# Attention products on the whole TensorE array, one PSUM bank per half, and the softmax shift cut as columns

## What is computed

```python
q = einsum('rc,bcn->brn', Wq, x) + bq        # 16 rows
k = einsum('rc,bcn->brn', Wk, x) + bk        # 16 rows
v = einsum('oc,bcn->bon', Wv, x) + bv        # 128 rows
attn = softmax(einsum('bri,brj->bij', q, k), axis=2)
x = gamma * einsum('bcj,bij->bci', v, attn) + x
```

## Time and profile before

| What | us |
|---|---|
| median of 3 runs | 207.81 (207.34 to 209.48) |
| the profiled execution, whole | 206.91 |
| its span, first to last instruction | 205.0 |
| PE, ACT, POOL, DVE busy | 192.7, 161.0, 155.9, 144.8 |

### The profile page before, as it was taken

The page is one execution under the profiler, slowest core; times in us unless marked ns, Lnnn a source line. Parts: engine busy times, 40 slices in busy tenths (PEclk is TensorE's granted clock), DMA queues, the critical chain, the costliest instruction groups (busy, mean ns, idle before and its releaser), DMA issues.

```text
span 205.0 us, 3349 instructions
## 1 busy us (share of the span) xinstructions
PE 192.7 (94%) x1217; PEld 124.8 (61%) x1217; DVE 144.8 (71%) x146; ACT 161.0 (79%) x237; POOL 155.9 (76%) x88
## 2 busy tenths in 40 slices
PE   7999999999889998999999999999999899998792
PEld 2433254555578656647875867775676768777570
DVE  0297688996999789689866897879874876532202
ACT  2229659889999989997999979699979997558420
POOL 1330000686499999998978988999999999999990
PEclk9998599999999999999999999999999999999998
DMA  6808000030040004002100004001410101001011
GB/s 184 328 14 205 0 2 3 13 93 0 3 106 0 2 6 102 0 6 51 51 3 3 0 2 107 0 6 51 102 53 5 51 0 51 30 28 51 3 51 51
DMA packets 3746, 9.31 MB, mean 45 GB/s; under 512 B 532, under 2 KB 916, under 8 KB 3732
## 3 DMA queue, kind: packets, MB, share of 16 engines
q1 hardware_dynamic: 3732, 9.12, 15.0%
HBM read 2.69 MB, written 2.10 MB: 23 GB/s over the span
## 4 chain that ended last, share of the span: by engine, by line
PE 51%; ACT 15%; POOL 15%; DVE 9%; issue 6%; DMA 2%; SPq 0%; POOLq 0%; DVEq 0%; ACTq 0%
PE out_psum L570 20%; POOL attn_lo L310 10%; PE ring L535 8%; ACT ring L344 7%; ACT attn L362 6%; PE out_psum L600 5%; POOL attn_hi L305 4%; PE out_psum L571 4%; DVE neg_max L435 4%; PE ring L521 4%; PE ring L511 3%; PE ring L556 3%; DMA qk_swapped<-qk 2%; PE ring L499 2%; DVE x_all L460 1%
## 5 line engine op out<-in xcount | busy, mean ns | idle before, releaser
L310 POOL TENSOR_TENSOR attn_lo<-attn,attn_hi 128x1024 fp32r<-128x1024 f32 x48 | 116.2, 2441 | 8.9 <-ACT attn_hi L369 8.0
L435 DVE TENSOR_REDUCE neg_max<-ring 128x1 f32<-128x1024 f32 x64 | 76.5, 1220 | 14.3 <-PE ring L537 13.5
L344 ACT ACTIVATE ring<-ring,neg_max 128x1024 f32<-128x1024 f32 x64 | 69.7, 1088 | 13.1 <-DVE neg_max L435 12.4
L362 ACT ACTIVATE attn<-ring 128x1024 f32<-128x1024 f32 x64 | 63.5, 1024 | 15.8 <-PE ring L558 15.4
L305 POOL TENSOR_SCALAR attn_hi<-attn 128x1024 fp32r<-128x1024 f32 x32 | 36.2, 1138 | 27.9 <-ACT attn L362 27.4
L556 PE MATMUL ring<-qk,qk_swapped 64*128 64x512 f32 x64 | 30.1, 485 | 2.7 <-ACT attn L362 2.0
L570 PE MATMUL out_psum<-attn_hi,v_hi 64*128 64x512 f32 x96 | 30.7, 399 | 1.5 <-DVE x_all L463 1.2
L571 PE MATMUL out_psum<-attn_hi,v_hi 64*128 64x512 f32 x96 | 30.7, 399 | 0.0
L558 PE MATMUL ring<-qk_swapped,qk 64*128 64x512 f32 x64 | 30.5, 491 | 0.0
L570 PE MATMUL out_psum<-attn,v 64*128 64x512 f32 x64 | 30.0, 588 | 0.0
L571 PE MATMUL out_psum<-attn,v 64*128 64x512 f32 x64 | 30.0, 588 | 0.0
(11 more groups left out here) (48 smaller groups left out, 322.4 us busy)
## 6 DMA issues: line engine op xcount, KB each, us to landing
qk_swapped<-qk SPq DMA_DIRECT2D x16, 256.0 KB, 3.7
out_dram<-x_all SPq DMA_DIRECT2D x8, 256.0 KB, 2.0
x_all<-x_in SPq DMA_DIRECT2D x3, 512.0 KB, 7.1
...
qk<-shift_rows SPq DMA_DIRECT2D x7, 8.0 KB
qk_swapped<-shift_rows SPq DMA_DIRECT2D x7, 8.0 KB
```

What stands on the lines that cost most here:

```text
L310: nc.gpsimd.tensor_tensor(attn_lo[:, k - 1], attn[:, k], attn_hi[:, k - 1].bitcast(fp32), ALU.subtract).then_inc(lo_made, 1)
L344: nc.scalar.activation(e[:], e[:], ACT.Exp, bias=max_column(s, i), accum_out=row_sum[s][:, i:i + 1]).then_inc(sum_made, 1)
L362: nc.scalar.activation(attn[:, k], ring_tile("ET", s, k)[:].rearrange("p (a n) -> p a n", a=2), ACT.Exp).then_inc(attn_made, 1)
L435: nc.vector.tensor_reduce(max_column(s, i), ring_tile("E", s, i)[:], axis=AX.X, op=ALU.max, negate=True).then_inc(max_made, 1)
```

## The change

Counts of entries in the order lists:

| Entry | before | after |
|---|---|---|
| PH, native PV, other PV (PE) | 48, 16, 48 | 46, 18, 46 |
| warm matmuls in the list (PE) | 31 | 23 |
| steps in PE_ORDER from full-array to row-split entries or back | 61 | 124 |
| of these, into a warm entry | 13 | 7 |
| hi, lo on POOL | 32, 48 | 33, 36 |
| hi on ACT; lo on DVE | 16; 0 | 13; 10 |
| v_hi on ACT, on POOL | 8, 0 | 1, 7 |
| v_lo on DVE, on POOL | 8, 0 | 2, 6 |
| mask and stack on DVE, on POOL | 7, 0 | 6, 1 |
| place on SP | 9 | 8 |

- Products (`WHOLE`, all stages): one matmul with 128 contraction rows and 512 columns in place of the pair, into the bank of the half. A half's products wait for the finish of the same half of the stage before. DVE's finish is one instruction.
- Stage 0 has four native k (0, 1, 4, 7).
- Shift: DVE subtracts the logarithm from the negative maximum and cuts the columns in two fp32r parts (`parts`, three small instructions); one fp32r matmul transposes them, and one copy brings the rows out of PSUM. ACT's copy of the maxima is gone.
- In stage 0, first half (`ADDED`), the rows are not placed by DMA: each of the four ETs is followed by eight small matmuls of 128 columns (64 rows each, in pairs) that add them. Their selection matrices and the identity are a new input (`units`), loaded by SP after `late` and rounded on POOL.
- QK.1 leaves PSUM by one ACT instruction (`evac`), and POOL masks and stacks it.
- All five lists are rearranged.

```diff
 PAIRS = [0, 1, 2, 3, 1, 2, 3, 0]
+NATIVES = [(0, 1, 4, 7), (0, 7), (0, 7), (0, 7), (0, 7), (0, 7), (0, 7), (0, 7)]
...
 BY_HALVES = (0,)
+ADDED = (0,)
+WHOLE = (0, 1, 2, 3, 4, 5, 6, 7)
+FROM_SBUF = (1,)
...
 PE_ORDER = """
-raw.0.0.0 raw.0.1.1 QK.1.0.2 E.0.2.0 E.0.1.1 warm.0.8 E.0.0.2 E.0.3.0 warm.0.2 E.0.4.1 warm.0.1 E.0.5.2 E.0.7.0
...
-ET.4.5.0 PH.3.6 PH.3.4 E.5.6.2 ET.4.7.0 PV.3.6 E.6.3.1 PV.3.4 PV.3.5 V.5.0.0 shift.5.1.2 PH.4.1 E.6.0.1 ET.4.0.0
-PH.4.3 PH.4.2 E.6.7.2 ET.4.6.0 PV.4.2 E.6.5.1 PV.4.3 PV.4.1 E.6.1.0 PV.4.0 ET.5.3.2 QK.7.0.1 ET.5.1.2 PH.4.6
...
-PH.7.2 PV.7.3 PV.7.0 PV.7.1 PV.7.2 ET.7.4.0 ET.7.7.2 PH.7.5 PH.7.6 PH.7.4 PV.7.7 PV.7.5 PV.7.6 PV.7.4
+raw.0.0.0 raw.0.1.1 QK.1.0.2 E.0.2.0 E.0.0.1 E.0.3.2 warm.0.4 E.0.1.0 E.0.7.1 E.0.4.2 warm.0.2 E.0.6.0 warm.0.2
+E.0.5.1 warm.0.1 shift.0.0.2 warm.0.4 E.1.0.0 E.1.7.2 warm.0.3 QK.2.0.1 ET.0.2.0 shift.0.1.2 warm.0.3 ET.0.1.2
...
+shift.5.1.2 PV.3.6 ET.4.1.0 E.6.7.2 ET.4.4.1 PV.4.0 V.5.0.0 ET.4.5.1 E.6.4.2 PH.4.6 E.6.1.0 E.6.2.1 PH.4.2 PH.4.1
+QK.7.0.2 ET.5.0.1 ET.5.1.0 PV.4.7 PV.4.1 ET.5.2.1 ET.5.6.2 E.6.3.0 PV.4.2 PH.4.3 PV.4.6 E.6.5.2 E.6.6.1 PH.4.5
...
+PV.7.3 PV.7.4 PH.7.1 PV.7.2 PV.7.1
...
+            nc.gpsimd.tensor_scalar(units[:], units32[:], 1.0, 0.0, ALU.mult, ALU.add).then_inc(units_made, 1)
...
             def log_sums(s, h):
...
-                nc.scalar.copy(neg[:, len(tiles):], neg[:, 0:len(tiles)]).then_inc(max_twice, 1)
...
+                nc.scalar.activation(log_sum[s][:, part], row_sum[s][:, part], ACT.Ln).then_inc(log_made, 1)
...
+            def attn_lo_of(s, k):
+                wait_for_cut(dve, "hi", s, k)
+                nc.vector.tensor_tensor(attn_lo[:, k - 1], attn[:, k], attn_hi[:, k - 1].bitcast(fp32),
+                                        ALU.subtract).then_inc(cut_made["lo", "vector"], 1)
...
+            def cut_shift(s, h):
...
+                nc.vector.tensor_tensor(shift[s][:, part], neg_max[s][:, part], log_sum[s][:, part],
+                                        ALU.subtract).then_inc(shift_made, 1)
+                dve.wait_ge(shift_made, nth_parts[s, h])
+                nc.vector.tensor_copy(hi, whole).then_inc(shift_hi_made, 1)
+                dve.wait_ge(shift_hi_made, nth_parts[s, h])
+                nc.vector.tensor_tensor(lo, whole, hi.bitcast(fp32), ALU.subtract).then_inc(shift_cut, 1)
...
             def shift_to_rows(s, h):
...
+                nc.vector.tensor_copy(rows_of(s, h)[:], ring_tile("shift", s, h)[0:rows, 0:P]
+                                      ).then_inc(shift_in_rows, 1)
...
             def finish(s, h):
...
+                if s not in WHOLE:
...
+                bank, x = (out_psum[:, part], x) if s in WHOLE else (out_psum[:, HALF:N], to)
+                nc.vector.scalar_tensor_tensor(out=to, in0=bank, scalar=gamma, in1=x,
                                                op0=ALU.mult, op1=ALU.add).then_inc(x_made, 1)
...
             def transpose_shift(s, h):
...
-                nc.tensor.matmul(to, both(neg_max, s, h), late[:, IDENTITY], start=True, stop=False)
-                nc.tensor.matmul(to, both(log_sum, s, h), late[:, IDENTITY + 1], start=False,
-                                 stop=True).then_inc(shift_mm, 1)
+                nc.tensor.matmul(to, parts, units[:, IDENTITY], start=True, stop=True).then_inc(shift_mm, 1)
...
             def energies_transposed(s, k):
...
+                if added(s, h):
+                    for t in range(SLOTS):
+                        stop, at = t == SLOTS - 1, slice(t * P, (t + 1) * P)
+                        nc.tensor.matmul(to[:, 0:HALF][:, at], units[0:64, SELECT + t], added_rows[h][0:64],
+                                         start=False, stop=stop)
+                        last = nc.tensor.matmul(to[:, HALF:N][:, at], units[64:128, SELECT + t], added_rows[h][64:128],
+                                                start=False, stop=stop)
...
-                    nc.tensor.matmul(out_psum[:, 0:HALF], v[0:64], a[0:64], start=start, stop=stop)
-                    last = nc.tensor.matmul(out_psum[:, HALF:N], v[64:128], a[64:128], start=start, stop=stop)
+                    if s in WHOLE:
+                        last = nc.tensor.matmul(out_psum[:, half_of(k)], v, a, start=start, stop=stop)
+                    else:
+                        nc.tensor.matmul(out_psum[:, 0:HALF], v[0:64], a[0:64], start=start, stop=stop)
+                        last = nc.tensor.matmul(out_psum[:, HALF:N], v[64:128], a[64:128], start=start, stop=stop)
...
             def wait_for_out(s, k):
...
+                if s in WHOLE:
+                    before = [(s - 1, h if s - 1 in WHOLE else 1)]
+                else:
+                    before = [(s, 0)] if h == 1 else [(s - 1, 0), (s - 1, 1)]
+                if before[0][0] >= 0:
+                    pe.wait_ge(x_made, max(nth_finish[b] for b in before))
```

More of the change, by code:

```diff
@@ L36 @@
[L36 to L40, removed]
@@ L58 @@
[L58 to L62, removed]
@@ L63 @@
[L63 to L67, removed]
@@ L69 @@
+attn.5.7 sum.7.4 sum.7.7 attn.6.6 attn.6.1 attn.6.3 sum.7.3 attn.6.5 sum.7.1 sum.7.2 attn.6.7 sum.7.6 sum.7.0 hi.6.1
+log.7.1 attn.6.2 attn.6.4 hi.6.4 attn.6.0 attn.7.5 attn.7.6 attn.7.1 attn.7.7 attn.7.2 attn.7.0 hi.7.6 attn.7.3
+hi.7.3 attn.7.4 hi.7.4 hi.7.1
 """
 DVE_ORDER = """
-mask.1.0 max.0.2 stack.1.0 max.0.1 max.0.0 max.0.3 max.0.4 max.0.5 max.0.7 max.1.6 max.1.4 rows.0.0 max.1.7 max.0.6
-v32.0.0 max.1.3 max.1.2 mask.2.0 stack.2.0 rows.0.1 max.1.5 max.1.0 v_lo.0.0 v32.1.0 max.1.1 max.2.2 max.2.6 max.2.4
@@ L78 @@
-mask.7.0 stack.7.0 max.6.6 max.6.2 max.6.4 finish.4.1 rows.6.1 v32.6.0 max.7.1 max.7.6 finish.5.0 max.7.4 v_lo.6.0
-max.7.0 max.7.3 finish.5.1 max.7.5 max.7.2 max.7.7 rows.7.1 finish.6.0 v32.7.0 v_lo.7.0 finish.6.1 finish.7.0
-finish.7.1
+max.0.2 max.0.0 max.0.3 max.0.1 max.0.7 max.0.4 parts.0.0 max.0.6 max.0.5 rows.0.0 max.1.0 max.1.7 parts.0.1
+mask.2.0 rows.0.1 stack.2.0 max.1.4 v32.0.0 max.1.1 max.1.6 v32.1.0 max.1.2 max.2.0 max.1.3 max.1.5 mask.3.0
+parts.1.1 stack.3.0 max.2.4 rows.1.1 max.2.5 max.2.7 max.2.2 max.3.4 max.3.2 max.2.1 finish.0.1 max.3.3 max.2.3
@@ new lines @@
+finish.0.0 max.2.6 v32.2.0 max.3.7 parts.2.1 rows.2.1 max.3.1 mask.4.0 stack.4.0 max.3.5 max.3.0 max.3.6 max.4.1
+max.4.3 finish.1.1 max.4.6 v_lo.2.0 finish.1.0 max.4.2 v32.3.0 parts.3.1 max.4.0 max.4.5 rows.3.1 max.4.4 mask.5.0
+stack.5.0 lo.2.2 max.4.7 max.5.1 max.5.2 finish.2.0 finish.2.1 parts.4.1 max.5.0 v32.4.0 rows.4.1 max.5.4 max.5.3
+mask.6.0 stack.6.0 max.5.5 max.5.7 max.5.6 max.6.0 parts.5.1 finish.3.0 rows.5.1 max.6.7 lo.4.3 finish.3.1 v32.5.0
+max.6.4 max.6.2 max.6.1 mask.7.0 stack.7.0 v_lo.5.0 max.6.3 max.6.5 max.6.6 max.7.5 finish.4.0 finish.4.1 parts.6.1
@@ L325, in _ @@
                     attn_hi_of(s, k)
+                elif what == "lo":
+                    attn_lo_of(s, k)
+                elif what == "v_hi":
+                    make_v_hi(s)
+                elif what == "v_lo":
+                    make_v_lo(s)
+                elif what == "mask":
+                    mask_from_sbuf(s)
                 else:
-                    attn_lo_of(s, k)
+                    stack_from_sbuf(s)
         @block.scalar
@@ L384, in _ @@
                     make_v_hi(s)
+                elif what == "evac":
+                    evacuate_qk(s)
                 else:
@@ L653 @@
         late[:, BV + l] = bv_l[None, :]
-    late[:, IDENTITY] = np.eye(P, dtype=f32)
-    late[:, IDENTITY + 1] = -late[:, IDENTITY]
+    units = np.zeros((P, UNITS, P), f32)
+    units[:, IDENTITY] = np.eye(P, dtype=f32)
+    for t in range(SLOTS):
+        for row in (t, SLOTS + t):
+            units[[row, 64 + row], SELECT + t] = 1.0
     late[:, LAYER1] = sets[QK_SETS]
@@ L664 @@
         "late_in": late,
+        "units_in": units,
     }
```

301 lines of the change are left out of this document (182 added, 119 removed).

## The result

The changed kernel takes 218.34 us (median of 4 runs, 216.44 to 219.06), the kernel before 207.57 beside it: a ratio of 1.049, 95% interval 1.039 to 1.059. The forecast was 210.5, slower, with 214.0 as the upper end. The direction came out, but the loss is 10.8 us where 2.7 were forecast, and the time is outside the range.

What follows compares the result with a forecast made beforehand. The prediction took PE and POOL as full from 60 us to the end. PE work +9.4, warm matmuls -1.7, waits -5.0, end -0.8 and +0.8 given back made +2.7 us: 210.5 us, range 200.5 to 214.0.

Steps and rivals of the forecast that it cites:

- nine `parts` of three small instructions, at most that 0.33 each: DVE's new cut of the shift: its small instructions add 8.9 us to DVE's work.
- DVE's 1.5 to 4 us of idle: DVE's idle time in each ten us, said to cover some 1 us of delayed maxima at each switch of work.
- rival (d): DVE's `lo` runs at 3.37 us each beside POOL and holds back maxima: slower by much, 215 us; chance 0.10.
- Waits, 14.0 to 9.0: PE's waits on other engines: fall by 5.0 us through the separate bank, lighter ACT and POOL and an earlier start.
- Cut products: Products on PE: 276 full-array matmuls at 0.216 us in place of the row-split pairs, -5.5 us.
- Switches: PE's changes between row-split and full-array entries: 63 more at 0.20 us each, +12.6 us.
- rival (c): A switch on PE costs only the 0.08 us of its first delay: faster, 202.9 us; chance 0.07.
- rival (e): Weight loads on PE's full array are not hidden, 0.19 us more for each of 276 products: 262 us; chance 0.02.
- DVE's `lo`: Ten `lo` instructions on DVE at 1.93 us each: +19.3 us of DVE work, 12.6 to 33.7.
- small pairs: Small matmuls behind the ETs of stage 0's first half, 0.12 us a pair: +1.9 us on PE, to 3.6.
- (a): POOL binds and the switches fall into PE's own waiting: faster, 200.1 us; chance 0.15.
- (b): Bank per half and moved cuts let PE's waits fall by 7 to 8 us: no change, 207.8 us; chance 0.24.

Runs made afterwards that it cites:

- u2: Changed kernel with the cut of the shift of stages 1 to 7 moved from DVE's list to POOL's: 211.05 us, ratio 1.017.
- w2: Changed kernel with the cut of the shift in stages 1 to 7 made of reductions, same place in DVE's list: 210.49 us, ratio 1.016.
- m1: Kernel before with series of matmuls added behind its last product, POOL and ACT idle: 233.36 us with the added work, not compared.
- u1: Changed kernel with its lists, but the shift of stages 1 to 7 made as before: 215.06 us, ratio 1.039.

## Why the prediction was wrong

- **The step that failed: "nine `parts` of three small instructions, at most that 0.33 each", with "DVE's 1.5 to 4 us of idle" as cover.** The bound of 0.33 came from the rows' cut, which reads PSUM. `parts` reads SBUF only, and beside POOL its instructions took up to 2.25 us. The rows said less than I took from them, too: the earlier trace rows have 1.1 of idle at 60 to 70 us, not 1.5, and between 90 and 100 us the trace has 0.8. Idle on average is no cover either: in stage 6 `v32` and the ring tile stood behind the cut, and PE behind both. The bare trace had a hint in the earlier trace rows: one form on DVE from 948 to 2527 ns, two inputs in SBUF. I read it for `lo` (rival (d)) and not for the small instructions. Nine cuts were put at 8.9 us, and seven took 13.3; but it is single instructions of up to 2.25 us ahead of the ring tile that cost, not the sum. By u2 and w2 the price is 7.3 to 7.9 us.
- **Waits, 14.0 to 9.0.** Once the hold is gone they fall further than forecast, from 15.4 (the balance's figure for before) to 7.4 and 8.6. In the changed kernel 14.9 are left: the hold took back what the rest of the change gave.
- **Cut products, mis-sized.** 0.216 was the nearest row, but of bf16. The form takes 0.228 to 0.231: 276 x 0.231 against 288 x 0.226 is -1.3 and not -5.5, a miss of 4.2 us.
- **Switches, right.** 63 x 0.20: the rows of the changed kernel and m1 (0.205) show it, and rival (c) falls. They are the largest cost of the change. Of the reason, that a load doesn't run beside the matmul before a switch, no run shows more than the length.
- **Lower clock, +1.8, not in the sum.** It falls in 160 to 180 us, behind the waits for the cut, and u1, u2 and w2 don't have it there. One execution of the changed kernel had a clock of 0.992 and took 216.44, the three at 0.976 took 218.1 to 219.1; in which part of the span they differ, no trace shows.
- **What bounds the kernel.** From 60 us on, PE and POOL were called full by four stretches. In all of them up to 200 us PE is busy for 8.8 to 10.0 of ten and POOL for 8.3 to 10.0, so the picture was right in the main and too smooth.
- **The rest.** Full-array loads are hidden: 0.231 a product with loads of 0.19, so rival (e) falls. DVE's `lo` takes 2.00 on average (forecast 1.93; one took 3.47), so (d) falls, though its time, 215, came nearest. The small pairs stand at 0.11 to 0.12, the end fell by 0.8, ACT and POOL fell as forecast within 2 us. Rivals (a) and (b) ask that the gains pay the switches; they don't.
- **The sum.** Forecast -5.5 + 3.4 - 3.0 + 1.9 - 1.7 + 12.6 - 5.0 + 0.8 - 0.8 = +2.7. Measured -0.9 (streams) + 12.6 - 0.5 (waits) + 1.8 (clock) - 0.8 = +12.2; the executions differ by 219.06 - 206.91 = 12.15. That w2 comes out at the forecast's 210.5 is two misses against each other: products 4.2 dearer, waits about 3 lower than taken. That is luck, and no support for the forecast.

Not isolated, so only argued: what `evac` with POOL's mask and stack, the rows added in stage 0 and the `v_hi` and `v_lo` on POOL bring each. Together with the new lists they are in w2's fall of the waits.
